# A tower of nine layers: combined projection weights, tile widths in the embedding and the dense experts, order of the gate products

## Chip, cores and metric

One core of one Trainium2 chip. The metric is the device time of one execution in microseconds. Three runs of the kernel before gave 907.95, 909.51 and 910.41; their median is 909.51.

## What is computed

A tower on T = 16 x 36 = 576 tokens of width 256: patch embedding, then four blocks of a sequence mixer and a feed-forward part, all fp32. What the change touches:

```python
# embedding
h = patches @ W.T + b                       # 768 -> 256
# second mixer, a selective state-space layer; x_in is the normed h
x, z = split(x_in @ W_in)                   # W_in 256 x 512
delta_raw, B, C = split(x @ W_x)            # W_x 256 x (256 + 16 + 16)
delta = softplus(delta_raw @ W_dt + b_dt)
h_n = scan(exp(delta * A_n), delta * x * B_n)   # n = 0..15
y = ((sum_n C_n h_n + x * D_param) * silu(z)) @ W_out
# its feed-forward part: 4 experts, all computed for all tokens
n1 = relu(layernorm(x @ W1[e] + b1[e]));  out_e = layernorm(n1 @ W2[e] + b2[e])
# third mixer
act = silu(conv(x_up));  f, i, hidden = grouped 4x4 products of act
# h = scan of functions of f, i, hidden;  out = ((h[-1] + skip * act) * silu(z)) @ w_down
```

## The kernel before

Each engine has its own hand-written program; semaphores join them. Tokens lie in NT = 5 tiles: four of 128 and the last of LAST = 64 (`TILE_N`). PS is PSUM with 8 banks; an fp32 product shows as two instructions in the trace. All products go through `mm` (line 428). `keep_warm(turns, root)` issues 4 idle products of zeros per turn and then waits for the VectorE step of a norm numbered `root`, and issues 5 more. `transpose_x` turns the normed tiles XH into XT (256 x 576, padded to 640 with zeros), which ScalarE's `xt_copy` takes out of PSUM (line 911 or 916) after the norm's square roots (line 901).

Embedding: `products_by_block` (lines 595 to 613) waits for block k of patches and weights and multiplies all five tiles. VectorE waits for the constants (`ld_const`, as do ScalarE at line 997 and GpSimd), adds the bias (1473) and takes statistics (1297).

State-space stage. TensorE (674 to 713): x and z from W_in, B and C from x, delta_raw from x, delta from its copy `dr`, then D_param * x, then the sums over C_n h_n as GpSimd (1229) delivers them. ScalarE (1030 to 1066): copies of x, SiLU of z, copies of B and C (1038), of delta_raw (1042), absolute value (1047), exponential (1050), logarithm (1052), exponential of A_log (1054), then the decays (1064), which it writes to PSUM. VectorE (1581 to 1628) makes softplus from them as max(v,0) + log(1 + exp(-|v|)) with a correction, dx = delta * x, then per state the input (1608) and two scans (1616). SyncE (392 to 406) stores B and C in DRAM when `bc_rows` is 2 and broadcasts them to all partitions, row by row.

Dense experts: per expert, `first_products` (bias of all pairs of tiles, then the tiles from XT), `second_products` of the expert before, `n1_transposes`. VectorE takes statistics (1652), ScalarE normalises (1081, 1092, 1104), GpSimd scales (1237), VectorE adds (1642). The last tile uses 64 columns of the array.

Third mixer: eight projections `up(m)` in two pairs of banks each (x for m < 4, z above), then per m `hidden(m)` and `gates_fi(m)`. HP(m) shares banks with the gates, so `hidden_read` and `gates_read` (VectorE, 1710 and 1715) hold TensorE back, and ScalarE's absolute values (1145), exponential (1147) and logarithm (1149) follow each pair of gates. Then `az_ready` products (840), idle products, `h2_ready` products (845), norm.

Between the embedding and the state-space stage lie a recurrent mixer, a norm (lines 1524 to 1532, TensorE's idle products at line 650) and routed experts. After the third mixer come routed experts, an LRU mixer and routed experts.

## Time and profile before

| | before |
|---|---|
| median of 3 runs | 909.51 us |
| profiled execution | 910.45 us |
| its span, first to last instruction | 908.6 us |
| mean granted TensorE clock | 0.92 of 2.4 GHz |
| TensorE, VectorE, ScalarE, GpSimd busy | 86, 38, 28, 15% of the span |
| embedding | 3.96 to 20.46 |
| first projection to first scan of the state-space stage | 246.15 to 281.13 |
| 16 states of the scan | 281.13 to 338.7 |
| dense experts, first bias to last statistics | 369.54 to 438.3 |
| gates of the third mixer to its output products | 471.57 to 492.94 |

Busy shares are averages over stages with different limits. In the time line, a row gives start and duration in us from the span's start, and in brackets how long the engine had been idle and what released it; PEld are TensorE's weight loads, which run ahead of its products. Rows of equal operations are merged, with their count.

### The profile page before, as it was taken

How to read it: one execution, taken by the hardware profiler on the slowest of the kernel's cores; microseconds unless marked ns; L12 is line 12 of the kernel's file. 1: busy time of each engine (PE TensorE's matmuls, PEld its weight loads, DVE VectorE, ACT ScalarE, POOL GpSimd, SP SyncE). 2: the span in 40 equal slices, each digit the busy share in tenths (PEclk: the TensorE clock that was granted, in tenths of full speed). 3: DMA queues.
4: the chain of work that ended last, by engine and by line, in shares of the span. 5: the costliest groups of instructions: out<-in, count | busy, mean ns of one | idle time of the engine just before them, and what ended most of it. 6: DMA issues, size and time to landing. Idle time of an engine off the chain costs nothing.

```text
span 908.6 us, 13681 instructions
## 1 busy us (share of the span) xinstructions
PE 785.4 (86%) x4875; PEld 599.0 (66%) x4954; DVE 349.3 (38%) x1002; ACT 250.1 (28%) x583; POOL 133.2 (15%) x100
## 2 busy tenths in 40 slices
PE   8878779999972668897896989999998988999997
PEld 5466439988541334564574558999984555999995
DVE  1434650000319996545765742111114551111113
ACT  1222114433243340436166122212220021122221
POOL 1000020000204991012204030000004012000004
PEclk9855889999995999799997979999999979999998
DMA  9500056995132532000000044999954024799972
GB/s 338 219 3 2 1 223 223 323 306 196 32 107 61 152 99 105 1 0 1 0 1 0 1 161 151 321 319 321 323 208 156 0 71 191 231 327 320 320 235 84
DMA packets 39590, 139.27 MB, mean 153 GB/s; under 512 B 5744, under 2 KB 20288, under 8 KB 27904
## 3 DMA queue, kind: packets, MB, share of 16 engines
q1 hardware_dynamic: 37312, 132.88, 43.4%
q0 software_dynamic: 2240, 5.90, 1.9%
q8 instruction: 22, 0.36, 0.2%
q14 instruction: 16, 0.13, 0.0%
HBM read 127.40 MB, written 11.35 MB: 153 GB/s over the span
## 4 chain that ended last, share of the span: by engine, by line
PE 66%; DVE 14%; DMA 5%; issue 5%; ACT 5%; POOL 3%; DVEq 0%; POOLq 0%; SPq 0%; ACTq 0%
PE PS L428 63%; DVE arena L1616 4%; POOL arena L1216 2%; DMA arena<-x_slots 1%; DVE stats L1297 1%; PE PS L485 1%; PE PS L451 1%; POOL arena L1229 1%; DMA arena<-y_slots,posu 1%; DMA arena<-w_moe 1%; ACT arena L1012 1%; DMA x_slots<-XH,posu 1%; ACT XT L911 1%; DMA y_slots<-arena 1%; DMA arena<-bc_scratch 0%
## 5 line engine op out<-in xcount | busy, mean ns | idle before, releaser
L428 PE MATMUL PS<-arena 128*128 128x128 f32 (+4 forms) x3348 | 421.6, 280 | 28.1 <-ACT arena L1012 9.8
L428 PEld LDWEIGHTS PS<-arena 128*128 128x128 f32 (+2 forms) x3348 | 368.7, 172 | 69.5 <-issue 18.3
L428 PE MATMUL PS<-warm 128*128 128x512 bf16 (+1 forms) x397 | 106.4, 379 | 14.8 <-DVE rs L1281 9.0
L1441 DVE TENSOR_TENSOR arena<-arena,PS 128x384 f32<-128x384 f32 (+1 forms) x62 | 30.3, 488 | 199.2 <-ACT arena L949 199.2
L428 PEld LDWEIGHTS PS<-warm 128*128 128x128 bf16 x476 | 46.4, 100 | 66.9 <-DVE rs L1281 12.9
L1216 POOL DMA_INDIRECT arena<-y_slots,posu x25 | 23.9, 954 | 384.6 <-DMA y_slots<-arena 377.9
L949 ACT ACTIVATE arena<-PS 128x384 f32<-128x384 f32 x62 | 30.4, 490 | 162.2 <-PE PS L428 162.2
L428 PE MATMUL PS<-arena,ident 128*128 128x512 f32 (+1 forms) x128 | 39.6, 456 | 38.1 <-POOL arena L1229 38.1
L1229 POOL TENSOR_TENSOR arena<-arena 128x1152 f32<-128x1152 f32 x16 | 56.1, 3509 | 48.8 <-DVE arena L1616 48.4
L1453 DVE SCALAR_TENSOR_TENSOR H<-arena,wgt,H 128x256 f32<-128x256 f32 (+1 forms) x25 | 11.9, 477 | 124.8 <-DMA arena<-y_slots,posu 124.4
L428 PEld LDWEIGHTS PS<-arena,ident 128*128 128x128 f32 x128 | 21.2, 196 | 56.6 <-POOL arena L1229 40.1
L1205 POOL DMA_INDIRECT x_slots<-XH,posu x25 | 24.1, 962 | 194.3 <-DVE posu L1401 187.6
L428 PE MATMUL PS<-XT,wsh 128*128 128x384 f32 (+1 forms) x144 | 43.0, 450 | 0.5 <-ACT arena L962 0.5
L901 ACT ACTIVATE dev<-rs 128x5 f32<-128x5 f32 x19 | 4.1, 216 | 140.5 <-DVE rs L1281 140.5
L1616 DVE TENSOR_TENSOR_SCAN arena<-PS,arena 128x576 f32<-128x576 f32 x32 | 41.6, 1341 | 0.0
L954 ACT ACTIVATE arena<-PS,arena 128x128 f32<-128x128 f32 x96 | 27.4, 368 | 45.5 <-PE PS L428 45.5
L428 PEld LDWEIGHTS PS<-XT,wsh 128*128 128x128 f32 x144 | 28.1, 209 | 13.1 <-issue 4.8
L1064 ACT ACTIVATE PS<-arena 128x560 f32<-128x560 f32 x32 | 23.3, 731 | 41.6 <-DVE arena L1616 37.3
L962 ACT ACTIVATE arena<-PS 128x256 f32<-128x256 f32 x43 | 16.5, 383 | 38.5 <-PE PS L428 38.5
L1237 POOL TENSOR_TENSOR arena<-arena,rowv 128x512 f32<-128x512 f32 (+1 forms) x12 | 13.6, 1158 | 87.5 <-ACT arena L1104 87.5
L428 PE MATMUL PS<-arena,wsh 128*128 128x384 f32 (+1 forms) x72 | 21.6, 426 | 2.9 <-DVE arena L1429 2.9
L485 PE MATMUL PS<-ident,arena 128*128 128x128 f32 x86 | 16.7, 276 | 7.9 <-DMA arena<-x_slots 5.7
(253 smaller groups left out, 756.1 us busy)
## 6 DMA issues: line engine op xcount, KB each, us to landing
arena<-w_moe SPq DMA_DIRECT2D x31, 1152.0 KB, 5.7
arena<-w_moe SPq DMA_DIRECT2D x31, 1024.0 KB, 5.2
arena<-w_moe SPq DMA_DIRECT2D x24, 1026.0 KB, 6.6
...
```

Source lines behind the costliest of these rows:

```text
L428: return nc.tensor.matmul(out_, l, r, start=start, stop=stop, skip_group_check=True)
L485: last = nc.tensor.transpose(PS[:, 6 + p, SB * d:SB * (d + 1)], xslot[p][:, 128 * d:128 * (d + 1)], ident[:, :])
L949: nc.scalar.activation(sg_s[x][:, 0:3 * SB], PS[:, 2 * x, 0:3 * SB], ACT.Silu)\
L954: last = nc.scalar.activation(hid_b[x][:, SB * c:SB * (c + 1)], PS[:, 2 * x, SB * c:SB * (c + 1)], ACT.Silu, bias=wbuf[p][:, o_ + c:o_ + c ...
L962: nc.scalar.activation(y_s[p], PS[:, 4 + p, 0:D], ACT.Copy).then_inc(sem("y_sb"), 1)
L1064: nc.scalar.activation(inner(dA[d]), inner(dl[:, d, :]), ACT.Exp, scale=A_s[:, d, bass.ds(n, 1)])\
L1205: pool.indirect_dma_start(x_slots, bass.IndirectOffsetOnAxis(ap=posu[0:TILE_N[j], k, j:j + 1], axis=0), tile(XH, j), None).then_inc(sem("s ...
L1216: pool.indirect_dma_start(Yg[0:TILE_N[j], k, j * D:(j + 1) * D], None, y_slots[0:SB * NBLK[name], :], bass.IndirectOffsetOnAxis(ap=posu[0: ...
L1229: nc.gpsimd.tensor_tensor(hC[:, n % 2, :, :], hs_[:, n % 2, :, :], bcC[:, n:n + 1, :].to_broadcast([128, KD, T]), ALU.mult)\
L1237: nc.gpsimd.tensor_tensor(u, u, row("g2", D, e)[0:TILE_N[j], None, :].to_broadcast([TILE_N[j], n, D]), ALU.mult)\
L1441: ins = v.tensor_tensor(hid_b[x][:, 0:full], sg_s[x][:, 0:full], PS[:, 2 * x + 1, 0:full], ALU.mult)
L1616: v.tensor_tensor_scan(hs_[:, n % 2, d], dA[d], dBx[:, n % 2, d], 0.0, ALU.mult, ALU.add)\
```

## The change

- Embedding: six idle products first; tiles 0 to 3 by block, the 64-token tile for all blocks at the end.
- State-space stage: TensorE forms W_x' = W_in[:, :256] W_x and W_dt' = W_x'[:, :256] W_dt on the chip, behind the first mixer's output products, in place of 8 of 11 turns of idle products; ScalarE copies them over wx_s and wdt_s. delta, then B and C, then x, then z come from XT. The step-size arithmetic runs in halves of 576 columns; z's copies come behind the first decays, its SiLU behind the loop.
- Dense experts: the last tile and its bias use all 128 columns; n1T is padded with zeros by VectorE.
- Third mixer: HP(m) has banks 2m, 2m+1; ScalarE copies hidden 0 and 1, VectorE 2 and 3; hidden 2 and 3 come before gates 1 to 3.

```diff
@@ -229,6 +229,11 @@
+        winT = YT[:, :, 0:D]
+        def XZ_PS(m):
+            return (PS[:, 0:2] if m else PS[:, 2:4])[:, :, 0:TH]
@@ -243,8 +248,8 @@
-        n1T = part(NT * D, KD, T)
-        eu = part(NT * D + KD * T, 2, NT, D)
+        n1T = part(NT * D, KD, NT * TT)
+        eu = part(NT * D + KD * NT * TT, 2, NT, D)
@@ -261,7 +266,7 @@
-            return PS[:, (0, 4)[m % 2]:(0, 4)[m % 2] + 2, 0:TH]
+            return PS[:, 2 * m:2 * m + 2, 0:TH]
@@ -609,12 +614,20 @@
-            products_by_block(PATCH_K, lambda k: pe.wait_ge(sem(f"ld_patch{k}"), 32),
-                              lambda k, j: patch_s[:, k, tsl(j)], lambda k: wtok_s[:, k, :])
+            pe.wait_ge(sem("warm_ready"), 1)
+            idle_products(6)
+            for k in range(PATCH_K):
+                pe.wait_ge(sem(f"ld_patch{k}"), 32)
+                for j in range(NT - 1):
+                    last = mm(TM(j), patch_s[:, k, tsl(j)], wtok_s[:, k, :], k == 0 and j % 2 == 0, k == PATCH_K - 1)
+                    if k == PATCH_K - 1:
+                        last.then_inc(sem("tm_ready"), 1)
+            for k in range(PATCH_K):
+                last = mm(TM(NT - 1), patch_s[:, k, tsl(NT - 1)], wtok_s[:, k, :], k == 0, k == PATCH_K - 1)
+            last.then_inc(sem("tm_ready"), 1)
...
-            pe.wait_ge(sem("warm_ready"), 1)
@@ -647,7 +660,33 @@
-            keep_warm(11, root=4)
+            def combined_weights():
+                pe.wait_ge(sem("ld_l1a"), 64)
+                for m in range(KD):
+                    for k in range(KD):
+                        last = nc.tensor.transpose(PS[:, 0, D * m + 128 * k:D * m + 128 * (k + 1)],
+                                                   win_s[:, k, 128 * m:128 * (m + 1)], ident[:, :])
+                last.then_inc(sem("wc_psum"), 1)
+                pe.wait_ge(sem("wc_copied"), 1)
+                for q in range(KD):
+                    for m in range(KD):
+                        last = mm(PS[:, 1, D * q:D * (q + 1)], wx_s[:, m, 128 * q:128 * (q + 1)], winT[:, m, :], m == 0, m == KD - 1)
+                last.then_inc(sem("wc_psum"), 1)
+                for k in range(KD):
+                    for m in range(KD):
+                        last = mm(PS[:, 2, 2 * NS * k:2 * NS * (k + 1)], winT[:, m, 128 * k:128 * (k + 1)],
+                                  wx_s[:, m, D:D + 2 * NS], m == 0, m == KD - 1)
+                last.then_inc(sem("wc_psum"), 1)
+                pe.wait_ge(sem("wc_copied"), 2)
+                for k in range(KD):
+                    for q in range(KD):
+                        last = mm(PS[:, 3, D * k:D * (k + 1)], wx_s[:, q, 128 * k:128 * (k + 1)], wdt_s[:, q, :], q == 0, q == KD - 1)
+                last.then_inc(sem("wc_psum"), 1)
+            combined_weights()
+            keep_warm(3, root=4)
+            pe.wait_ge(sem("wc_copied"), 4)
@@ -669,36 +708,26 @@
-            pe.wait_ge(sem("ld_l1a"), 64)
...
-            for m in range(2 * KD):
+            def from_xt(outs, w_of, done):
...
-                        last = mm(PS[:, 4 + 2 * (m % 2) + h, 0:TH], win_s[:, k, 128 * m:128 * (m + 1)], XT[:, k, hsl(h)],
-                                  k == 0, k == KD - 1)
-                last.then_inc(sem("xz_psum"), 1)
+                        last = mm(outs[h], w_of(k), XT[:, k, hsl(h)], k == 0, k == KD - 1)
+                last.then_inc(sem(done), 1)
+            for m in range(KD):
+                from_xt([PS[:, 4 + 2 * m + h, 0:TH] for h in range(2)], lambda k: wdt_s[:, k, 128 * m:128 * (m + 1)], "dt_psum")
+            from_xt([PS[0:2 * NS, h, 0:TH] for h in range(2)], lambda k: wx_s[:, k, D:D + 2 * NS], "bc_psum")
+            for m in range(2 * KD):
...
-                    pe.wait_ge(sem("xz_read"), 2)
...
-            last.then_inc(sem("bc_psum"), 1)
+                    pe.wait_ge(sem("bc_rows"), 2)
+                if m >= 2:
+                    pe.wait_ge(sem("xz_read"), m)
+                from_xt([XZ_PS(m)[:, h, :] for h in range(2)], lambda k: win_s[:, k, 128 * m:128 * (m + 1)], "xz_psum")
...
-            for m in range(KD):
...
-            pe.wait_ge(sem("bc_rows"), 2)
@@ -722,7 +751,7 @@
-                mm(PS[0:TILE_N[j], bank, 0:n * D].rearrange("p (j d) -> p j d", d=D), ones_b[:, 0:TILE_N[j]], b_, True, False)
+                mm(PS[:, bank, 0:n * D].rearrange("p (j d) -> p j d", d=D), ones_b[:, :], b_, True, False)
@@ -731,9 +760,9 @@
-                        z = PS[0:TILE_N[j], q, (j % 2) * D:(j % 2 + 1) * D]
+                        z = PS[:, q, (j % 2) * D:(j % 2 + 1) * D]
...
-                            last = mm(z, XT[:, k, tsl(j)], wl1_s[:, 0, e, k, :], False, k == KD - 1)
+                            last = mm(z, XT[:, k, TT * j:TT * (j + 1)], wl1_s[:, 0, e, k, :], False, k == KD - 1)
@@ -758,9 +787,9 @@
-                        z = PS[0:TILE_N[j], 4 + q, (j % 2) * D:(j % 2 + 1) * D]
+                        z = PS[:, 4 + q, (j % 2) * D:(j % 2 + 1) * D]
...
-                            last = mm(z, n1T[:, k, tsl(j)], wl1_s[:, 1, e, k, :], False, k == KD - 1)
+                            last = mm(z, n1T[:, k, TT * j:TT * (j + 1)], wl1_s[:, 1, e, k, :], False, k == KD - 1)
@@ -776,6 +805,7 @@
+            pe.wait_ge(sem("n1_pad"), 1)
@@ -807,31 +837,29 @@
-                if m < 2:
-                    pe.wait_ge(sem("z_read"), 2 * m + 1)
-                else:
-                    pe.wait_ge(sem("gates_read"), m - 1)
+                pe.wait_ge(sem("z_read"), m + 1)
...
-                pe.wait_ge(sem("hidden_read"), m + 1)
-                if m < 2:
-                    pe.wait_ge(sem("z_read"), 2 * m + 2)
+                pe.wait_ge(sem(("hidden_act", "hidden_dve", "gates_read", "gates_read")[m]), (2, 2, 1, 2)[m])
...
-            for m in range(2 * KI - 1):
+            for m in range(KI + 2):
...
-            up(2 * KI - 1)
+            up(KI + 2)
+            hidden(1)
+            up(KI + 3)
...
+            hidden(2)
+            hidden(3)
...
-                hidden(m)
@@ -1018,7 +1046,19 @@
-            xt_copy("ffn0", "rms_w", norms=3)
+            act.wait_ge(sem("wc_psum"), 1)
+            nc.scalar.activation(winT, PS[:, 0, :].rearrange("p (m i) -> p m i", m=KD), ACT.Copy).then_inc(sem("wc_copied"), 1)
+            square_root()
+            act.wait_ge(sem("wc_psum"), 3)
+            nc.scalar.activation(wx_s[:, :, 0:D], PS[:, 1, :].rearrange("p (q i) -> p q i", q=KD), ACT.Copy)\
+                .then_inc(sem("wc_copied"), 1)
+            nc.scalar.activation(wx_s[:, :, D:D + 2 * NS], PS[:, 2, 0:KD * 2 * NS].rearrange("p (k c) -> p k c", k=KD), ACT.Copy)\
+                .then_inc(sem("wc_copied"), 1)
+            act.wait_ge(sem("wc_psum"), 4)
+            nc.scalar.activation(wdt_s[:, :, :], PS[:, 3, :].rearrange("p (k f) -> p k f", k=KD), ACT.Copy)\
+                .then_inc(sem("wc_copied"), 1)
+            xt_copy("ffn0", "rms_w", norms=2)
@@ -1027,42 +1067,46 @@
-            for m in range(4):
...
-                                     ACT.Copy if m < 2 else ACT.Silu).then_inc(sem("xz_read"), 1)
+            nc.scalar.activation(A_s[:, :, :], colv[:, COL["A_log"]:COL["A_log"] + KD * NS]
+                                 .rearrange("p (k n) -> p k n", k=KD), ACT.Exp).then_inc(sem("A_exp"), 1)
+            for m in range(KD):
+                act.wait_ge(sem("dt_psum"), m + 1)
+                nc.scalar.activation(hs_[:, 1, m].rearrange("p (h t) -> p h t", h=2), PS[:, 4 + 2 * m:6 + 2 * m, 0:TH], ACT.Abs,
+                                     bias=col("b_dt", m)).then_inc(sem("dt_abs"), 1)
+                act.wait_ge(sem("dt_abs"), m + 1)
+                nc.scalar.activation(hs_[:, 0, m], hs_[:, 1, m], ACT.Exp, scale=-1.0).then_inc(sem("dt_e"), 1)
...
-            act.wait_ge(sem("dr_psum"), 1)
...
-            act.wait_ge(sem("dt_psum"), 1)
+            def xz_copy(m):
+                act.wait_ge(sem("xz_psum"), m + 1)
+                dst = xs[:, m, :] if m < 2 else zs[:, m - 2, :]
+                nc.scalar.activation(dst.rearrange("p (h t) -> p h t", h=2), XZ_PS(m), ACT.Copy).then_inc(sem("xz_read"), 1)
...
-                nc.scalar.activation(hs_[:, 1, m].rearrange("p (h t) -> p h t", h=2), PS[:, 4 + m:8:2, 0:TH], ACT.Abs,
...
-                                 .rearrange("p (k n) -> p k n", k=KD), ACT.Exp).then_inc(sem("A_exp"), 1)
+                act.wait_ge(sem("dt_u"), m + 1)
+                nc.scalar.activation(dBx[:, 1, m], dBx[:, 0, m], ACT.Ln).then_inc(sem("dt_ln"), 1)
+                xz_copy(m)
...
-            act.wait_ge(sem("delta_ready"), 1)
...
-            with act.Fori(0, NS) as n:
+            def decays(n):
...
-                    act.wait_ge(sem("delta_ready"), 1)
+                    act.wait_ge(sem("delta_ready"), d + 1)
...
+            decays(0)
+            for m in range(KD, 2 * KD):
+                xz_copy(m)
+            with act.Fori(1, NS) as n:
+                decays(n)
+            nc.scalar.activation(zs[:, :, :], zs[:, :, :], ACT.Silu).then_inc(sem("z_silu"), 1)
@@ -1126,15 +1170,23 @@
-            for m in range(KI):
-                x_copy(m)
+            def hidden_copy(m):
+                act.wait_ge(sem("h_psum"), m + 1)
+                nc.scalar.activation(two(df[:, m, :]), HP(m), ACT.Copy).then_inc(sem("hidden_act"), 1)
...
+            x_copy(0)
+            x_copy(1)
+            x_copy(2)
...
+            x_copy(3)
...
+            z_silu(1)
+            hidden_copy(0)
...
-            z_silu(1)
...
+            hidden_copy(1)
@@ -1150,7 +1202,7 @@
-                act.wait_ge(sem("hidden_read"), m + 1)
+                act.wait_ge(sem("hidden_act" if m < 2 else "hidden_dve"), m % 2 + 1)
@@ -1578,27 +1630,33 @@
-            dve.wait_ge(sem("dt_abs"), KD)
+            ee, u, ln_u = hs_[:, 0], dBx[:, 0], dBx[:, 1]
...
-                mark(v.tensor_scalar(dr[:, m, :].rearrange("p (h t) -> p h t", h=2), PS[:, 4 + m:8:2, 0:TH],
-                                     col("b_dt", m), None, ALU.add))
-            join()
+                dve.wait_ge(sem("dt_abs"), m + 1)
+                v.tensor_scalar(dr[:, m, :].rearrange("p (h t) -> p h t", h=2), PS[:, 4 + 2 * m:6 + 2 * m, 0:TH],
+                                col("b_dt", m), 0.0, ALU.add, ALU.max).then_inc(sem("dt_relu"), 1)
+                dve.wait_ge(sem("dt_e"), m + 1)
+                v.tensor_scalar(u[:, m], ee[:, m], 1.0, None, ALU.add).then_inc(sem("dt_u"), 1)
+                dve.wait_ge(sem("dt_u"), m + 1)
+                link(v.scalar_tensor_tensor(ee[:, m], u[:, m], 1.0, ee[:, m], ALU.subtract, ALU.subtract))
+                dve.wait_ge(sem("dt_relu"), m + 1)
+                mark(v.tensor_tensor(dl[:, m], dr[:, m], ee[:, m], ALU.subtract))
+            dve.wait_ge(sem("A_exp"), 1)
+            v.tensor_scalar(A_s[:, :, :], A_s[:, :, :], -1.0, None, ALU.mult).then_inc(sem("A_ready"), 1)
+            dve.wait_ge(sem("xz_read"), 1)
...
-            ee, u, ln_u = hs_[:, 0], dBx[:, 0], dBx[:, 1]
...
-            dve.sem_inc(sem("scan_half"), 2)
+            for m in range(KD):
+                dve.wait_ge(sem("dt_ln"), m + 1)
+                link(v.scalar_tensor_tensor(ln_u[:, m], u[:, m], 1.0, ln_u[:, m], ALU.is_gt, ALU.mult))
+                v.tensor_tensor(dl[:, m], dl[:, m], ln_u[:, m], ALU.add).then_inc(sem("delta_ready"), 1)
+                if m == 0:
+                    dve.sem_inc(sem("scan_half"), 2)
+            for m in range(KD):
+                dve.wait_ge(sem("delta_ready"), m + 1)
+                dve.wait_ge(sem("xz_read"), m + 1)
+                mark(v.tensor_tensor(dx[:, m], dl[:, m], xs[:, m], ALU.mult))
+            join()
@@ -1626,6 +1684,7 @@
+            dve.wait_ge(sem("z_silu"), 1)
@@ -1634,6 +1693,7 @@
+            v.memset(n1T[:, :, T:NT * TT], 0.0).then_inc(sem("n1_pad"), 1)
@@ -1707,7 +1767,7 @@
-                v.tensor_copy(two(df[:, m, :]), HP(m)).then_inc(sem("hidden_read"), 1)
+                v.tensor_copy(two(df[:, m, :]), HP(m)).then_inc(sem("hidden_dve"), 1)
@@ -1720,13 +1780,10 @@
-            hidden_copy(0)
+            hidden_copy(2)
+            hidden_copy(3)
...
-                if m + 1 < KI and m == 0:
-                    hidden_copy(1)
...
-                if 1 <= m and m + 1 < KI:
-                    hidden_copy(m + 1)
```

## Rows read from the trace of the kernel before

**Rows 1.** The page: clocks granted in 40 slices; shares of the last chain

```profile
PEclk9855889999995999799997979999999979999998
...
PE 66%; DVE 14%; DMA 5%; issue 5%; ACT 5%; POOL 3%; DVEq 0%; POOLq 0%; SPq 0%; ACTq 0%
```

**Rows 2.** Time line, embedding: start us, us, engine, line, operation, tiles, count, [idle<-releaser]

```profile
3.96 3.06 PEld L428 LDWEIGHTS PS<-arena 128*128 128x128 f32 x8 [3.96 <-DMA arena<-w_tok]
...
12.87 0.19 PEld L428 LDWEIGHTS PS<-arena 128*64 128x64 f32 x2 [0.33 <-issue]
...
15.37 0.19 PEld L428 LDWEIGHTS PS<-arena 128*64 128x64 f32 x2 [0.33 <-issue]
...
16.47 0.20 ACT L997 ACTIVATE lru_c<-colv 128x1 f32<-128x1 f32 x1 [14.47 <-DMA gatew<-gate_w]
```

**Rows 3.** Chain in order of time, after the embedding: start us, us, what

```profile
20.48 1.09 DVE H L1473 x3
21.59 1.74 DVE stats L1297 x5
```

**Rows 4.** Time line, TensorE's weight loads in the third block's projections

```profile
452.72 13.39 PEld L428 LDWEIGHTS PS<-XT,arena 128*128 128x128 f32 x56 [0.52 <-issue]
...
466.17 0.92 PEld L428 LDWEIGHTS PS<-arena 128*128 128x128 f32 x4
```

**Rows 5.** Time line, TensorE's idle products before the second norm

```profile
89.95 9.44 PE L428 MATMUL PS<-warm 128*128 128x512 bf16 x33 [0.16 <-issue]
...
102.13 1.25 PE L428 MATMUL PS<-warm 128*128 128x512 bf16 x5 [2.74 <-DVE rs L1281]
```

**Rows 6.** Time line, setup of the state-space stage

```profile
246.15 4.12 PE L428 MATMUL PS<-XT,win_s 128*128 128x288 f32 x16 [0.36 <-ACT XT L911]
...
248.37 0.65 ACT L1034 ACTIVATE arena<-PS 128x576 f32<-128x576 f32 x1 [2.36 <-PE PS L428]
...
255.09 1.59 PEld L428 LDWEIGHTS PS<-arena,wx_s 128*32 128x32 f32 x8 [0.39 <-issue]
...
257.25 0.69 ACT L1038 ACTIVATE arena<-PS 32x288 f32<-32x288 f32 x2 [1.41 <-PE PS L428]
...
281.13 2.60 DVE L1616 TENSOR_TENSOR_SCAN arena<-PS,arena 128x576 f32<-128x576 f32 x2
```

**Rows 7.** Groups by line and shape, 246 to 281.2: busy us, mean ns | idle before

```profile
L1592 DVE SCALAR_TENSOR_TENSOR arena<-arena 128x1152 f32<-128x1152 f32 x1 | 1.4, 1359 | 0.0
...
L1050 ACT ACT_TABLE_LOAD x1 | 1.3, 1283 | 0.0
...
L1050 ACT ACTIVATE arena<-arena 128x1152 f32<-128x1152 f32 x1 | 1.2, 1162 | 0.0
```

**Rows 8.** The four broadcasts of B (line 396): issue to landing

```profile
DMA to landing us min/median/max: 3.2/5.6/6.5
```

**Rows 9.** Time line, one pass of the dense experts

```profile
405.67 0.11 PEld L428 LDWEIGHTS PS<-bias_p,ones_b 128*128 128x128 bf16 x2 [0.39 <-issue]
...
411.09 0.85 PEld L749 LDWEIGHTS PS<-ident,arena 128*128 128x128 f32 x8 [0.38 <-ACT arena L1081]
```

**Rows 10.** Chain in order of time, two steps of the dense experts

```profile
400.31 10.85 PE PS L428 x46
...
413.26 10.85 PE PS L428 x46
```

**Rows 11.** Time line, gate products of the third block and what follows

```profile
471.57 1.19 ACT L1145 ACTIVATE arena<-PS 128x576 f32<-128x576 f32 x2
...
472.79 1.16 ACT L1147 ACTIVATE arena<-arena 128x1152 f32<-128x1152 f32 x1
...
490.11 1.19 ACT L1145 ACTIVATE arena<-PS 128x576 f32<-128x576 f32 x2 [3.62 <-PE PS L428]
...
492.94 11.67 PE L428 MATMUL PS<-arena 128*128 128x256 f32 x40 [2.87 <-DVE arena L1715]
...
508.01 9.97 PE L428 MATMUL PS<-arena 128*128 128x256 f32 x40
```

40 lines of the change are left out of this document (removed).

## Prediction

> **What bounds the kernel now.** I read the page first: its chain of work that ended last is two thirds TensorE, the rest VectorE, DMA and ScalarE, and its row of granted clocks shows stretches of half speed [rows 1]. The shares are averages over nine stages, so the stages that the change touches were read one by one: the time line, to see on which engine each gap ends, then the chain in order of time. They give four different limits. The embedding is TensorE alone: one row of it runs from 3.96 without a gap [rows 2], and VectorE's last three additions and the statistics follow [rows 3]. The setup of the state-space stage is a relay: from the first projection at 246.15 to the first scan at 281.13 pass 34.98 us, in which TensorE, ScalarE and VectorE wait for one another [rows 6]. The dense experts are TensorE for 10.85 of every 12.95 us [rows 10]. The gate products of the third block are a ring of three engines, four turns from 471.57 to the next stage at 492.94 [rows 11]. What these stages lose or gain reaches the end in full: each hands its result to a layer norm on which all later work waits, and the later stages are unchanged.
>
> **Embedding.** Five tiles of tokens, the last of 64, are multiplied block by block. An fp32 product is two instructions, so a block is 10. One block runs from 12.87 to 15.37, 2.50 us [rows 2]. In a row of products of one width 56 instructions of 288 columns take 466.17 - 452.72 = 13.45, 0.240 each [rows 4]; by columns that is 0.2135 for 256, and 2.13 for ten. A block with the narrow tile in it so pays 0.37 for turning to 64 columns and back. The change does the narrow tile for all blocks at the end. In front come six idle products of 512 columns, between the zeroing of their operand (about 1.3 us) and the arrival of the first block at 3.96; the first eight weight loads took 3.06, so nearly twice the later pace, and I take 2.1 for them with the engine already busy (bounds: eight at 0.2135, 1.7; and 3.5). Sum: 3.96 + 2.1 + 5 x 1.71 + 12 x 0.2135 + 0.2 for one turn = 17.4. The constants land at 16.47 [rows 2]; the additions of tiles 0 to 3 run from there at 0.36 each [rows 3] and the last ends at 18.4, where statistics started at 21.59. **Gain 3.1**, between 1.5 (cold start, blocks arriving late; then it is DMA that is next) and 3.2 (the constants bound it).
>
> **Combined weights.** W_in's first half times W_x, and that times W_dt, are now formed on the chip: 4 transposes, 4 products of 256 columns, 4 of 32, 4 of 256, and four copies on ScalarE, in place of 32 of the 44 idle products behind the first mixer. VectorE works alone there until 102.13, where TensorE's idle products came to an end at 99.4 and it sat idle for 2.74 [rows 5]. At the upper clock: transposes to 91.2, copy to 91.9, 16 instructions to 94.9, copy to 95.6, 8 to 97.4, copy to 98.0, twelve idle ones to 100.0: cover 2.1 us. ScalarE has nothing else there but a root of 0.2. I book **0**; the bounds are a gain of 1.5, if a shorter idle time leaves the transposes at 103.9 at the upper clock, and a loss of 4.1, if all of it runs at the lower one (rival 3). The wait for the four weight loads moves here from 246; they were issued by 12.5, and this is at 90.
>
> **State-space setup.** Before: x, then B and C, then the low projection, a copy, the step-size projection, six serial steps over 1152 columns. After: the step size comes straight from XT, so TensorE starts with it. Times in the frame of before, from 246.15:
> - TensorE: the two halves of dt are 16 instructions of 288 columns, 3.84; the first half is on ScalarE at 248.37, as x was [rows 6]. B and C follow; their copies lay 257.25 - 255.09 = 2.16 behind the load [rows 6], now 250.1 + 2.2 = 252.4, and are done at 253.1. x, first half, 8 instructions behind them, arrives at 254.5.
> - ScalarE: absolute value and exponential of each half, 0.65 to 0.75 each, end at 249.8 and 251.7; B and C copies 253.1; a table load of 1.28, whose follower starts with no idle time [rows 7]; logarithm and x copy of half 0 to 255.75; of half 1 to 257.1; load, first decays 258.4 to 259.9.
> - VectorE: dt's bias, u, e - u and their difference, per half at most 0.77 + 3 x 0.68 (half of 1.36, [rows 7]), run from 249.1 to 254.6, in the shadow. It then waits for the x copy at 255.75 (the zeros of the decays share its bank), then six steps of 0.7 to 260.1 and two inputs of 1.36: first scan at 263.0.
> - SyncE: B and C leave for the scratch at 253.2; the broadcasts start 1.7 later and land 3.2 to 6.5 after issue [rows 8]: B0 by 258, B1 by 260 to 262.3, against a need at 261.7. Late next after VectorE, by at most 0.6.
>
> 281.13 - 263.0 = **18.1**, bounds 14 and 18.5. z's two halves are copied behind the first decays; TensorE has them at 262.5, ScalarE is free at 263.2, and the second decays are wanted at 264.3: 1.1 of cover. z's SiLU moves behind the loop, where ScalarE idles. The 16 turns of the loop are VectorE's, unchanged.
>
> The Trainium skill (ScalarE: Activation LUTs, What ACT_TABLE_LOAD costs) gives each switch a drain of 1.38 behind the 1.28. By it the two switches in the new relay would cost 2.8 more on ScalarE. The rows show no such idle time, so the trace decides.
>
> **Dense experts.** The last tile is computed 128 wide, on zeros. From a bias load to the transposes behind the products lie 411.09 - 405.67 = 5.42 us [rows 9], for 1280 bias columns (0.53) and 20 instructions of 256 (4.27): 4.80 without turns. So 0.6 is lost in each pass. There are 8; the first is partly at the lower clock (0.5), and in the last the biases are paced by ScalarE (0.35). The step of 12.95 becomes 10.85 - 1.2 + 2.1 [rows 10], as VectorE's and ScalarE's part starts 0.6 earlier too; the added zeroing of 128 columns is over before the logits. Sum 0.5 + 6 x 0.6 + 0.35 = **4.4**, bounds 1.8 (only 0.1 for each narrow product and for each bias) and 4.8.
>
> Against it the Trainium skill (TensorE: Matmul & The Clock Gate, LDWEIGHTS) lets a weight load cost its columns over 1.2 GHz. Doubling the narrow ones adds an estimated 0.053 us to each of 32, 1.7 in all, if they lay open. In a row of one width they don't: 0.240 is the columns' own time [rows 4].
>
> **Gate products.** Before, a copy, the gates' absolute values and two VectorE steps stood between one turn and the next. After, all four hidden products have banks of their own. TensorE: eight projections, hidden 0 and 1, gates 0 are 80 instructions, over at 472.3 as before; hidden 2 and 3 to 474.3, VectorE's copy to 475.1, gates 1 to 477.2. ScalarE, 1.19 + 1.16 + 1.16 a turn [rows 11]: absolute values at 472.4, 477.2, 480.8, 484.4. Then 1.19 and two VectorE steps of 0.77: the next stage at 487.15 instead of 492.94, **5.8** earlier. What follows is TensorE's and moves with it; its start at the lower clock (40 instructions in 11.67 against 9.97 later, [rows 11]) stays. ScalarE's hidden copies fit between waits. Bounds 3 (a SiLU or copy in the new order late by one projection, and the clock down longer) and 6.5.
>
> **Sum.** 3.1 + 0 + 18.1 + 4.4 + 5.8 = 31.4. The profiled execution took 910.45, with a span of 908.6; that makes 879.05 and 877.2. It lies 0.94 above the median of the runs; on the median I forecast **878.1**.
>
> **Rivals.**
> 1. The turns are cheap (the row shows only 0.1 where a full pair of loads follows) and the first block stays cold: 1.5 + 18.1 + 1.8 + 5.8 = 27.2, so 882.3. Against it: the two rates of rows 2 and 4.
> 2. The new relay is slower than drawn: ScalarE holds nine steps in one order, and one that is late moves all. With the x copies behind both logarithms' waits, broadcasts at 6.5, and z on the second decays, it gives 14: 882.2.
> 3. The combined weights end up on the path: all at 1.2 GHz, TensorE reaches the transposes at 107.9 instead of 103.86: 4.1 back, 882.2. For it: half a microsecond's gaps for each copy; against it: 16 products in a row, and 2.1 of cover.
> 4. Slower than before: the shift sets TensorE's idle gaps otherwise, and the long routed stages, which are bound by it, run at 1.2 GHz where they had 2.4. A microsecond there costs half of one, so it decides from 63 us more of it. The mean of 0.92 means some 145 us below now. At 80 us more: 909.5 - 31.4 + 40 = 918. Against it: those stages have 9s in the row of clocks [rows 1], and nothing in them is changed.
> 5. It doesn't do what it says: the next late thing takes the whole gain of one part, as when the first scan waits for something unseen. Half of 31.4: 894.
>
> **Chances.** Forecast 0.62 (875 to 881), rival 1 0.13, 2 0.10, 3 0.06, 5 0.07, 4 0.02. Between the bounds of all parts the gain is 1.5 - 4.1 + 14 + 1.8 + 3 = 16 and 3.2 + 1.5 + 18.5 + 4.8 + 6.5 = 34.5; not all ends meet, so the range is 874 to 887, which leaves out 4, 5 and some of what combines. 0.3% is 2.7 us, about what measuring this kernel can tell from no change: faster 0.97, same 0.01, slower 0.02.
>
> **What would show it.** Statistics at 18.4; no 128*64 loads in the experts and a step of 11.7; idle products over before the root at about 99; 17 us from first projection to first scan; absolute values of the gates 3.6 apart. It is wrong if the first scan comes later than 20 us after the projections, if TensorE is the releaser of the first transposes of the second norm, or if the steps of the experts stay above 12.5.

## The result and the profile after

The changed kernel takes 878.67 us (median of 4 runs, 873.46 to 886.24), the kernel before beside it 908.73 (4 runs, 904.72 to 910.41): a ratio of 0.968, 95% interval 0.9637 to 0.9722. In two more series the ratio was 0.9611 (0.9554 to 0.9668) and 0.9659 (0.9629 to 0.9689). The forecast was 878.1, with a range of 874 to 887. So the total was met, by 30.1 us of gain in the medians against 31.4 in the sum. Two of its terms were not met, in opposite directions: the experts gave 7.2 us where 4.4 were booked, the gates 3.5 where 5.8 were. Most of what follows is about them.

The profiled execution after took 880.7, with a span of 878.9. The clocks granted in 40 slices, and the shares of the last chain, against [rows 1]:

```profile
PEclk9855889999999999899989899999999888999998
...
PE 60%; DVE 13%; DMA 11%; issue 5%; ACT 5%; POOL 3%; SPq 1%; DVEq 0%; POOLq 0%; ACTq 0%
```

TensorE's share of the chain fell from 66% to 60%, DMA's rose from 5% to 11%. Behind the first six slices the row before had a 5 (273 to 295 us: end of the setup, first scans) and four 7s, among them one in the experts (363 to 386 us); after, nothing there is below 8.

**Embedding** (against rows 2 and 3). TensorE's weight loads (start us, us, engine, line, operation, count, idle before), and then the chain:

```profile
3.88 2.46 PEld L433 LDWEIGHTS PS<-arena 128*128 128x128 f32 x8 [0.74 <-DMA arena<-w_tok]
6.61 8.50 PEld L433 LDWEIGHTS PS<-arena 128*128 128x128 f32 x40 [0.28 <-DMA arena<-w_tok]
15.45 2.35 PEld L433 LDWEIGHTS PS<-arena 128*64 128x64 f32 x12 [0.33 <-issue]
```

```profile
9.19 7.88 DMA gatew<-gate_w
...
17.10 1.75 DVE H L1525 x5
...
18.87 1.73 DVE stats L1349 x5
```

The narrow tile's twelve instructions stand in one row. TensorE is past them at 18.2 (17.4 in the sum), and the statistics start at 18.87 in place of 21.59: 2.7 earlier. As the bound said, the constants are now next late; they arrived at 17.10.

**Second norm** (against rows 5). TensorE's idle products:

```profile
94.01 2.54 PE L433 MATMUL PS<-warm 128*128 128x512 bf16 x9
99.54 1.25 PE L433 MATMUL PS<-warm 128*128 128x512 bf16 x5 [2.99 <-DVE rs L1333]
```

The combined weights are over before 94.01, the norm is still released by VectorE's root (`DVE rs`), and TensorE waits 2.99 where it waited 2.74. They cost nothing.

**State-space setup** (against rows 6). TensorE's first two groups, VectorE's last steps:

```profile
240.57 4.15 PE L433 MATMUL PS<-XT,wdt_s 128*128 128x288 f32 x16 [0.27 <-ACT XT L939]
244.65 2.13 PE L433 MATMUL PS<-XT,wx_s 128*32 128x288 f32 x8
```

```profile
250.12 0.74 DVE L1651 SCALAR_TENSOR_TENSOR arena<-arena 128x576 f32<-128x576 f32 x1
...
254.49 2.63 DVE L1666 TENSOR_TENSOR arena<-arena 128x1152 f32<-128x1152 f32 x2
257.03 2.60 DVE L1674 TENSOR_TENSOR_SCAN arena<-PS,arena 128x576 f32<-128x576 f32 x2
```

From first projection to first scan: 257.03 - 240.57 = 16.46 us, where it was 34.98. VectorE waited 0.98 for ScalarE's copy of x and is busy without a gap from 250.12 on: it bounds the start of the scans, as drawn. (The chain names a broadcast there, landing at 256.95, so 0.08 us ahead of the scan. VectorE had no idle time, so it was not late, but a faster VectorE would gain no more than these 0.08.)

**Dense experts** (against rows 10), two steps of the chain:

```profile
371.30 9.82 PE PS L433 x46
...
383.06 9.83 PE PS L433 x46
```

The step is 11.76 (11.75 in the sum), where it was 12.95.

**Gates** (against rows 11). ScalarE's absolute values, and what follows on TensorE:

```profile
439.93 1.19 ACT L1197 ACTIVATE arena<-PS 128x576 f32<-128x576 f32 x2
...
444.82 1.19 ACT L1197 ACTIVATE arena<-PS 128x576 f32<-128x576 f32 x2 [1.30 <-PE PS L433]
...
448.31 1.17 ACT L1197 ACTIVATE arena<-PS 128x576 f32<-128x576 f32 x2
...
451.77 1.17 ACT L1197 ACTIVATE arena<-PS 128x576 f32<-128x576 f32 x2
```

```profile
454.58 12.46 PE L433 MATMUL PS<-arena 128*128 128x256 f32 x40 [4.73 <-DVE arena L1775]
```

Four turns are 4.9, 3.5, 3.5 and 2.8 apart (4.8, 3.6, 3.6, 2.7 in the sum). The next stage begins 34.44 us behind the first projection, where it was 40.22: 5.8 less.

By these landmarks the two profiled executions differ so, 29.7 us in all: 2.7 in the embedding, 0.2 lost at the second norm, 3.0 in the first routed stage, 18.5 in the setup, 0.6 at the fourth norm, 8.0 in the experts, 5.0 from there to the norm of the next routed stage, 0.7 lost up to the seventh norm, and 7.2 lost from the last norm to the end. The experts gave more than booked, and the end, in which nothing was changed, lost.

### The profile page after: what moved, and what is told of

It is laid out like the page before. It is cut to its first block, busy times and chain, and to the rows that moved or that the text cites. A ratio compares the mean times of both kernels' runs of the same rounds, so it can differ in the third digit from the quotient of the medians.

```text
span 878.9 us, 13652 instructions
## 1 busy us (share of the span) xinstructions
PE 771.4 (88%) x4869; PEld 598.1 (68%) x4940; DVE 348.2 (40%) x1007; ACT 253.7 (29%) x590; POOL 132.8 (15%) x100
## 4 chain that ended last, share of the span: by engine, by line
PE 60%; DVE 13%; DMA 11%; issue 5%; ACT 5%; POOL 3%; SPq 1%; DVEq 0%; POOLq 0%; ACTq 0%
PE PS L433 57%; DVE arena L1674 4%; DMA arena<-w_moe 3%; DMA arena<-x_slots 3%; POOL arena L1268 2%; DVE stats L1349 1%; PE PS L490 1%; DMA arena<-bc_scratch 1%; PE PS L456 1%; POOL arena L1281 1%; DMA arena<-y_slots,posu 1%; DMA gatew<-gate_w 1%; SPq L319 1%; ACT arena L1040 1%; DMA x_slots<-XH,posu 1%
## 5 line engine op out<-in xcount | busy, mean ns | idle before, releaser
L433 PE MATMUL PS<-warm 128*128 128x512 bf16 (+1 forms) x379 | 102.7, 384 | 15.9 <-DVE rs L1333 9.4
L433 PEld LDWEIGHTS PS<-warm 128*128 128x128 bf16 x450 | 44.2, 101 | 65.5 <-DVE rs L1333 13.2
L977 ACT ACTIVATE arena<-PS 128x384 f32<-128x384 f32 x62 | 30.4, 490 | 169.1 <-PE PS L433 169.1
L990 ACT ACTIVATE arena<-PS 128x256 f32<-128x256 f32 x43 | 16.5, 383 | 38.5 <-PE PS L433 38.5
L490 PE MATMUL PS<-ident,arena 128*128 128x128 f32 x86 | 17.4, 286 | 7.7 <-DMA arena<-x_slots 5.5
L433 PE MATMUL PS<-arena,wsh 128*128 128x384 f32 (+1 forms) x72 | 21.6, 426 | 2.9 <-DVE arena L1481 2.9
```

What stands on the lines that cost most here:

```text
L433: return nc.tensor.matmul(out_, l, r, start=start, stop=stop, skip_group_check=True)
L490: last = nc.tensor.transpose(PS[:, 6 + p, SB * d:SB * (d + 1)], xslot[p][:, 128 * d:128 * (d + 1)], ident[:, :])
L977: nc.scalar.activation(sg_s[x][:, 0:3 * SB], PS[:, 2 * x, 0:3 * SB], ACT.Silu)\
L990: nc.scalar.activation(y_s[p], PS[:, 4 + p, 0:D], ACT.Copy).then_inc(sem("y_sb"), 1)
```

## The experiments

Twelve more runs were made, two of them of the changed kernel again. For each, one execution was profiled; its stretches are set side by side here (us). All limits are instructions that every kernel has: "setup" runs from the third norm's first copy into XT (ScalarE) to the first scan, "experts" from the first product (or its weight load) with the experts' weights to the next norm's copy into XT, "gates" from the first projection of the third block to the table load behind the gates, "behind" from there to the next norm's copy, "end" from the last norm's copy to the end.

| kernel | first XT | second to third XT | setup | experts | gates | behind | end |
|---|---|---|---|---|---|---|---|
| before | 26.38 | 139.36 | 36.54 | 80.48 | 40.99 | 29.6 | 176.4 |
| after | 23.66 | 136.40 | 17.93 | 72.53 | 35.24 | 30.4 | 183.6 |
| r1 after again | 24.02 | 135.20 | 17.93 | 75.23 | 35.24 | 30.6 | 178.0 |
| r2 embedding alone | 23.62 | 135.74 | 36.55 | 80.51 | 38.73 | 29.6 | 176.8 |
| r3 combined alone | 26.96 | 135.32 | 17.97 | 80.45 | 38.73 | 29.6 | 179.0 |
| r4 experts alone | 27.07 | 138.05 | 36.55 | 73.13 | 39.42 | 29.6 | 178.9 |
| r5 gates alone | 26.06 | 136.48 | 36.55 | 80.52 | 35.24 | 29.6 | 178.4 |
| r6 all but experts | 24.32 | 133.94 | 17.93 | 80.87 | 35.25 | 29.6 | 180.5 |
| r7 no warm start | 25.47 | 133.23 | 17.93 | 73.14 | 35.25 | 30.5 | 181.0 |
| r8 longer warm | 23.85 | 132.91 | 17.93 | 73.22 | 35.25 | 30.5 | 179.4 |
| r9 after, third | 24.05 | 135.94 | 17.93 | 73.39 | 35.25 | 30.5 | 178.3 |
| r10 ranks' gaps filled | 23.51 | 132.70 | 17.93 | 72.77 | 35.24 | 30.5 | 182.7 |
| r11 two gaps filled | 23.83 | 133.42 | 17.93 | 71.78 | 35.24 | 28.0 | 178.2 |
| r12 all filled | 23.62 | 133.09 | 17.93 | 71.63 | 35.24 | 28.0 | 183.0 |

**1. The same kernel again.** No edit.

> The changed kernel itself, so that the parts are weighed beside it on one chip. Its gain came out at 30 us instead of 31.4, and two stages don't match the sum: the stage of the dense experts was 4 us better than worked out, and the last routed feed-forward (739.76 to 852.74) lost 7 us to waits for the weight transfers. Theory 1, the loss varies from execution to execution: the time lies at 875 to 886, and the last routed feed-forward of this trace lasts anything between 106 and 114 us. Theory 2, the loss belongs to the change (the weights are fetched at another phase): the stretch lasts 112 to 114 us again, with waits of 7 us or more for w_moe.

Measured: 877.8 us (874.84 to 882.02) against 910.35. The end took 178.0 us, where the same kernel had taken 183.6. Leaving out experiments 10 and 12, which put idle products into this stretch, all profiles have the same code there, and it took 176.4 to 183.6. The stretch in whole, of the profiled execution after, of this one, and of the kernel before (us; busy time and instructions of TensorE, its weight loads, VectorE, ScalarE, GpSimd; the mean granted clock, DMA share, GB/s):

```profile
695.29:878.87 183.58, 168.24 (x1060) 145.37 (x1058) 38.73 (x123) 35.28 (x80) 18.98 (x20) 0.94 0.65 220
```

```profile
702.22:880.18 177.96, 163.51 (x1060) 142.75 (x1058) 38.72 (x123) 35.12 (x80) 18.99 (x20) 0.96 0.68 227
```

```profile
732.18:908.59 176.41, 164.15 (x1060) 143.13 (x1058) 38.74 (x123) 35.07 (x80) 18.97 (x20) 0.95 0.67 229
```

Theory 1 holds for most of it: the stretch varies from execution to execution. But the waits for weights, to which the expectation lays the loss, are not what differs. Of the 5.6 us between the two executions of the changed kernel, 4.7 are TensorE busy for longer with the same 1060 instructions (168.24 against 163.51), at a mean granted clock of 0.94 against 0.96; the time in which it is not busy differs by 0.9, and its waits for `w_moe` are 1.8 and 1.6. The GB/s are the same bytes over the two lengths, and explain nothing. Against the kernel before, of the 7.2 us 4.1 are busy time and 3.1 are not. How much of those 7.2 is the change stays open: the four kernels without the combined weights took 176.4 to 178.9 at the end (before, 2, 4, 5), the eight with them, 10 and 12 again left out, 178.0 to 183.6. The means are 2.1 us apart.

**2. The embedding alone.**

```
-            products_by_block(PATCH_K, lambda k: ..., lambda k, j: patch_s[:, k, tsl(j)], lambda k: wtok_s[:, k, :])
+            pe.wait_ge(sem("warm_ready"), 1)
+            idle_products(6)
+            ... blocks over tiles 0 to 3, then all blocks of tile 4
```

> The kernel before with the embedding part alone (twelve narrow loads, warm-up first, products in the new order). My sum: first statistics 2.7 to 3.1 us earlier, the rest unchanged, so 2.7 to 3.1 us faster than the kernel before. Rival: a gain ahead of the routed stages is swallowed by the wait for the expert weights, which are fetched at their own time: then the time is within 1 us of the kernel before although the first statistics come 2.7 us earlier.

Measured: 907.28 against 910.35, ratio 0.9976 (0.9943 to 1.0009), and the first XT at 23.62. Over all profiles the first XT comes at 26.06 to 27.07 without this part and at 23.51 to 24.32 with it and the warm start. In the means (26.6 and 23.8) that is a gain of 2.8. The time agrees (3.1), but its interval holds zero as well, so the time alone decides nothing between the sum and the rival. The stretches speak against the rival: the next two are no longer than in other kernels.

**3. The combined weights and the setup alone.**

```
+            combined_weights()
+            keep_warm(3, root=4)
...
-                last.then_inc(sem("dr_psum"), 1)
+                from_xt([...], lambda k: wdt_s[:, k, 128 * m:128 * (m + 1)], "dt_psum")
```

> The kernel before with the combined weights and the short state-space setup alone. My sum: first scan about 18.5 us after the first projection's start is saved, transposes of the second normalisation unmoved, 17.5 to 19 us faster. Rival, what is saved there is partly given back in the second routed feed-forward by waits for w_moe: 11 to 14 us faster, with the loss in the last 150 us of the trace.

Measured: 894.82 against 910.35, 15.5 us, ratio 0.9818 (0.9763 to 0.9872; that is 11.7 to 21.6 us). The setup is 17.97 in place of 36.54, to 0.04 us the same in every kernel that has this part, and the time from the first XT to the second is 79.15. Without this part it was 78.85, 79.06, 79.06 and 80.51 (before, 2, 4, 5), with it 78.8 to 80.1 in the other profiles: a cost of making the weights can't be told from this scatter. The setup's 18.6 is in the interval of the time; the rival, part of it given back at the end, isn't excluded, since the lower end of the interval is 11.7 and this kernel's end took 179.0 against 176.4.

**4. The full-width experts alone.**

```
-                mm(PS[0:TILE_N[j], bank, 0:n * D].rearrange("p (j d) -> p j d", d=D), ones_b[:, 0:TILE_N[j]], b_, True, False)
+                mm(PS[:, bank, 0:n * D].rearrange("p (j d) -> p j d", d=D), ones_b[:, :], b_, True, False)
... and the products' operands likewise 128 tokens wide
```

> The kernel before with the full-width dense experts alone (128 columns of every product, also in the last tile). My sum from the column counts: 4.4 us. The trace of the changed kernel showed 8.6 in this stage. If the full width itself brings more than I worked out (the switches of the tile's width cost more than I took), the gain is 7 to 9 us with the granted clock of the stage as in the kernel before. If 4 of the 8.6 came from the granted clock falling for a shorter time, at another phase of the kernel, this kernel shows the old dips and gains 4 to 5 us.

Measured: 904.72 against 910.35, ratio 0.9921 (0.9894 to 0.9948), so 4.7 to 9.6 us; the stage 73.13 in place of 80.48. It reaches the experts when the kernel before does (369.7 against 370.7 us) and still gains 7.35.

**5. The gates alone.**

```
-            gates_fi(0)
-            hidden(2)
...
+            hidden(1)
+            up(KI + 3)
+            gates_fi(0)
+            hidden(2)
+            hidden(3)
+            for m in range(1, KI):
+                gates_fi(m)
```

> The kernel before with the gate part alone (the gate products of the third block in one run with their functions' tables loaded less often). My sum said 5.8 us, and the traces of before and after differ by 5.75 from the first gate product to the table load behind the gates (40.99 us before, 35.24 after). But the kernels that left the gates alone took 38.73, 38.73 and 39.42 us there, with shorter stretches at the lower clock than the profiled run of before. Theory 1, the part is worth what I summed, 5 to 6 us. Theory 2, 2.3 us of it was the lower clock in the profiled run of before, from whose rows I worked: this kernel shows 35.2 us in that stretch and is 3 to 4 us faster than the kernel before in the mean of many runs.

Measured: 906.6 against 909.99, 3.4 us, ratio 0.9953 (0.9924 to 0.9981). That is 1.7 to 6.9 us and holds both theories; the stretches decide between them. (The tables are not loaded less often, as the expectation says: both orders have three loads there.) The stretch is 35.24, as in every kernel with this part. What it replaces took 38.73 twice, 39.42 and, in the profile that I had, 40.99. Two rows of ScalarE's absolute values in run 2, the third and the fourth turn:

```profile
475.67 1.19 ACT L1153 ACTIVATE arena<-PS 128x576 f32<-128x576 f32 x2 [3.05 <-PE PS L428]
...
481.40 1.19 ACT L1153 ACTIVATE arena<-PS 128x576 f32<-128x576 f32 x2 [2.15 <-PE PS L428]
```

In the profile before, the fourth waited 3.62 [rows 11], and the third 3.84. Theory 2: from the first turn to the fourth pass 16.27 here and 18.54 there, and the 2.3 between them are these two waits of ScalarE for TensorE. Over the whole stretch TensorE had 7.7 us at 1.2 GHz there and 4.5 here.

**6. All but the experts.** The changed kernel with the hunk of experiment 4 taken back.

> The changed kernel with the dense experts' tiles left at 64 columns in the last block. It reaches the experts at the phase of the changed kernel. If the narrow tile itself makes the lower clock last longer, the stretch from the first product of the expert stage to the next normalisation takes 79 to 81 us with 17 us or more of it at the lower clock, as in the three kernels that had narrow tiles, against 72.5 to 75.2 us with 10.2 to 13.7 in the three that had full ones; the whole is then 6 to 8 us slower than the changed kernel. If the phase decides, the stretch takes 76 to 78 us with 10 to 14 us at the lower clock, and the whole is 4 to 5 us slower.

Measured: 884.85 against 909.99 (ratio 0.9721, 0.9651 to 0.9792), a gain of 25.1 where the changed kernel gained 30.1 to 32.5. The stage is 80.87. Its first 20 us and then the rest, beside run 4 (columns as above; the clock is the third from the end):

```profile
344.38:364.38 20.00, 17.85 (x65) 12.24 (x64) 9.98 (x45) 7.19 (x16) 0.00 (x0) 0.74 0.00 1
364.38:394.38 30.00, 28.47 (x131) 19.19 (x130) 18.49 (x84) 15.51 (x38) 6.33 (x6) 1.00 0.00 1
394.38:425.25 30.87, 24.37 (x101) 13.64 (x100) 19.06 (x62) 10.03 (x24) 7.24 (x6) 0.89 0.00 1
```

```profile
369.76:389.76 20.00, 17.85 (x78) 13.38 (x77) 11.82 (x57) 7.27 (x17) 0.00 (x0) 0.83 0.00 1
389.76:419.76 30.00, 26.79 (x139) 22.14 (x137) 20.11 (x88) 20.01 (x49) 6.35 (x6) 1.00 0.00 1
419.76:442.79 23.03, 18.13 (x79) 10.17 (x80) 15.29 (x48) 5.40 (x15) 7.23 (x6) 0.93 0.00 0
```

This settles width against phase, the time at which the kernel reaches the stage. Five kernels with the narrow tile took 80.45 to 80.87, though they came to the stage at anything between 344 and 371 us; seven with full tiles took 72.5 to 75.2, 73.3 in the mean (and two with a gap filled, below, 71.6 and 71.8). The width is worth 7.2. From the clocks of the rows, 2 x ((1 - 0.74) x 20 + (1 - 0.89) x 30.87) = 17.2 us of run 6's stage were at 1.2 GHz, and 2 x ((1 - 0.83) x 20 + (1 - 0.93) x 23.03) = 10.0 of run 4's. By the same working the other narrow ones had 17 us, and the kernel before 20; the full ones 10, and run 1 14. The full width shortens the time at the lower clock by 7 us as a rule, at either phase. Why the clock is granted otherwise, the rows don't tell: the loads and products are as many, only wider.

**7. Without the idle products at the start.**

```
             pe.wait_ge(sem("warm_ready"), 1)
-            idle_products(6)
```

> The changed kernel without the six idle products at the start. If the embedding's products pay for a cold start, they end later than the constants arrive (17.1 us) and the first copy into XT comes 0.5 to 1.5 us later than 23.7. If the start is bound by the loads, as the chain says, the first copy into XT comes within 0.3 us of 23.7 and the time is that of the changed kernel.

Measured: 882.37 (ratio 0.9689, 0.9622 to 0.9757), first XT at 25.47, 1.6 later than in the mean of the kernels with them. The chain of this kernel shows TensorE where the constants were:

```profile
4.97 15.23 PE PS L433 x59
...
20.68 1.73 DVE stats L1348 x5
```

By this one profile the idle products are worth more than half of the embedding's gain. In the prediction that was the lower bound of 1.5, "cold start": here it is 26.6 - 25.5 = 1.1, against the mean of the four kernels without this part. The time line shows what they do: without them the weight loads start 0.43 us apart until 9.46 and 0.22 apart from there; in the kernel after, behind idle products from 1.30 on, that half pace ends at 5.71. The profile's granted clock reads 1.00 over both pieces, so this slow start can't be seen in it.

**8. A longer filling behind the combined weights.**

```
-            keep_warm(3, root=4)
+            keep_warm(7, root=4)
```

> The changed kernel with seven turns of idle products behind the combined weights in place of three, so that they end at about 99.5 instead of 96.6 us, when the second normalisation releases the next ones. If the transposes of the second normalisation (0.64 us a pair, at the lower clock in both kernels) pay for that gap, they take about half and the logits come 1 to 2 us earlier than 105.4. If the gap is not what keeps the clock low there, the transposes keep their 0.64 us and nothing moves, or the idle products end after 99.5 and cost up to 0.5 us.

Measured: 873.27 against 909.99, ratio 0.9574 (0.951 to 0.9639). TensorE ahead of the second norm's transposes, and the first of them:

```profile
94.32 7.29 PE L433 MATMUL PS<-warm 128*128 128x512 bf16 x33
101.89 0.41 PE L456 MATMUL PS<-ident,XH 128*128 128x128 f32 x2 [0.28 <-DVE XH L1359]
```

A pair of transposes takes 0.38 to 0.41 where it took 0.64 in both kernels. (In run 7, with the same gap of 2.99 unfilled, only the first pair took 0.63, the others 0.38 to 0.39: what the gap costs differs from one execution to the next.) The logits come only 0.6 earlier (104.78 against 105.37, though this execution was 0.2 later at the first XT), since the copies into XT set the pace then. The gain on the kernel before is 36.7 us, where the changed kernel had 30.1 to 32.5 in its three series. The second to third XT is 132.91, against 135.2 to 136.4 in the three profiles of the changed kernel. I had not expected that, and can't put it down to this edit alone, since runs 6 and 7 show 133.9 and 133.2 without it; but all four kernels with this filling lie at 132.7 to 133.4.

**9. The changed kernel beside its versions.** No edit.

> The changed kernel once more, beside three versions of it. 875 to 880 us. By the traces so far its stages repeat to 0.3 us (17.93 us from the second normalisation's XT to the first scan, 67.2 to 67.4 us behind the gates), and the two parts that don't are the stretches in which routed blocks wait for weights (177 to 184 us at the end) and the expert stage (72.5 to 75.2 us, by one more stretch of 3.4 us at the lower clock).

Measured: 881.47 (879.1 to 883.18) against 913.75. The stages repeated as said.

**10. The gaps ahead of the ranks filled,** and the filling of experiment 8.

```
+                idle_products(6)
                 pe.wait_ge(sem("masks"), STAGE[name] + 1)
```

> The changed kernel with seven turns of idle products behind the combined weights and six idle products in each of the three gaps between the gate logits and the ranks (2.4 to 2.55 us, ended by the masks of VectorE). In the traces each gap is followed by 7 to 10 us at the lower clock in the shared experts. If TensorE's idleness in the gap brings the clock down, the lower stretches behind 492 and 702 us are gone or halved and each saves 2 to 4 us; the kernel is 3 to 8 us faster than the changed one. If the clock falls there for another reason, the stretches stay as they are and the time is within 2 us of it.

Measured: 876.45, ratio 0.96 (0.9557 to 0.9643), 5.0 less than run 9. In the profiles 3.2 of it lie between the second and third XT (132.70 against 135.94), where both experiment 8's filling and the first of these gaps are; the run can't part them. Of the two lower stretches behind the later gaps one stayed and one went: the first 16 us behind the norm of each, first in this kernel, then in run 9 (columns as above).

```profile
484.45:500.45 16.00, 14.91 (x62) 9.56 (x61) 8.44 (x52) 5.14 (x8) 3.44 (x4) 0.79 0.26 81
694.39:710.39 16.00, 13.66 (x66) 8.68 (x65) 8.50 (x52) 5.14 (x8) 3.89 (x4) 1.00 0.28 97
```

```profile
486.85:502.85 16.00, 13.18 (x56) 9.11 (x55) 8.38 (x52) 5.14 (x8) 3.45 (x4) 0.79 0.25 78
698.91:714.91 16.00, 13.18 (x57) 9.08 (x56) 8.60 (x52) 5.15 (x8) 3.43 (x4) 0.79 0.25 81
```

The expectation of 2 to 4 us for each fell. What TensorE still waited for the masks was 0.83 us where the clock fell and 1.24 where it stayed up, so the length of what is left of the gap doesn't decide it. The end took 182.7 all the same, against 178.3 in run 9: at the higher clock (0.97 against 0.96) TensorE was not busy for 18.1 us of it, against 14.9. The longest of these waits, 4.17 us behind a VectorE product, stands in run 9 as well (4.12); what made the others longer stays open.

**11. Two longer gaps filled,** and the filling of experiment 8.

```
+                if e == E1:
+                    idle_products(15, 0)
...
+            pe.wait_ge(sem("gates_read"), KI - 1)
+            idle_products(14, 0)
+            mm(PS[:, 0, 0:512], warm[:, 0:128], warm[:, 0:512]).then_inc(sem("az_warm"), 1)
             pe.wait_ge(sem("gates_read"), KI)
...
             act.wait_ge(sem("gates_read"), KI)
+            act.wait_ge(sem("az_warm"), 1)
```

> The changed kernel with seven turns behind the combined weights, fifteen idle products in the gap of 4.73 us ahead of the products behind the gates (they follow at the lower clock, 6.8 us long) and fifteen in the gap of 3.50 us ahead of the last expert's second products (3.4 us at the lower clock follow). If the gaps bring the clock down, the expert stage loses its stretch at 53 us (72.5 to 73.2 us becomes 71 to 72) and the one behind the gates goes too; what the latter is worth depends on whether the down products wait for VectorE anyway: 0 to 3 us. In all 1 to 5 us faster than the changed kernel. If the clock falls for another reason, no change within 1 us.

Measured: 875.78 (871.8 to 879.76), ratio 0.9596 (0.9561 to 0.9631), 5.7 less than run 9. TensorE behind the gates in this kernel:

```profile
447.34 3.41 PE L433 MATMUL PS<-warm 128*128 128x512 bf16 x15 [1.26 <-DVE arena L1781]
450.80 10.07 PE L433 MATMUL PS<-arena 128*128 128x256 f32 x40
```

The same 40 products took 12.46 in the changed kernel, behind a gap of 4.73; now 10.07. The whole stretch from the gates to the next norm shrank by 2.5, all of it on the path, and the experts by 1.6 (73.39 to 71.78). For both gaps the first theory holds, in the stretches.

**12. All of it, and the gate weights off the list of constants.**

```
-            load(gatew[:, :, :, :], gate_w, "const")
+            load(gatew[:, :, :, :], gate_w, "gatew")
... and the waits for the constants from 16 * 6 to 16 * 5
```

> The changed kernel with all of these fillings, and with the gate weights off the list of constants for which VectorE waits at the start (17.10 us now; without them the wait ends at the fifth constant, some 0.5 us earlier, and the last embedding product at about 18 us is next late). If the pieces add: 4 to 12 us faster than the changed kernel, so 866 to 875 us, with the first statistics 0 to 0.5 us earlier. If a filled gap only moves the lower stretch to the next place, less than the sum of the two kernels before it.

Measured: 876.36 (870.44 to 878.65), ratio 0.9581 (0.9545 to 0.9617). The first XT came at 23.62, 0.2 to 0.4 earlier than in runs 8 and 9. But run 10 had 23.51 without this edit, so it shows nothing for it. Nothing came on top of run 11: the pieces don't add in the time, though the experts (71.63) and the stretch behind the gates (28.0) keep theirs; the end took 183.0. Against the changed kernel beside them, runs 10 to 12 are 5.0, 5.7 and 5.1 us faster, which the runs don't tell apart from one another. But experiment 8's filling alone had 36.7 us on the kernel before in its series, and these three have 37.3, 38.0 and 37.4 in theirs. So the longer filling behind the combined weights may carry all that the time shows; the 4.1 us of experiment 11 are shown in its stretches, not in the time.

## Why the prediction was right, and where it wasn't

**Embedding, 3.1 booked (its own times, 21.59 - 18.4, give 3.2), 2.7 to 2.8 measured.** Right in kind. The first eight loads took 2.46, where I took 2.1; TensorE is over at 18.2, not 17.4, and the constants arrive at 17.10, not 16.47. The gain stayed inside its bounds of 1.5 and 3.2. The price of a turn, 0.37 a block, is what the sum rests on: with full tiles only, 40 loads took 8.50, 0.2125 each, as worked out from the 0.2135 of a row of one width.

**Combined weights, 0 booked.** Right: no cost stands out of the scatter of 78.8 to 80.5 us between the first two XTs. The cover was drawn as 2.1 and is 2.99: TensorE was past them at 94.0 plus twelve idle products. Rival 3 (all of it at 1.2 GHz) did not come up. The upper bound, transposes at the upper clock, took four more turns of idle products (experiment 8), and was worth 0.6 to the logits, not 1.5.

**Setup, 18.1 booked, 18.5 measured** (18.6 from XT). It lies at the upper bound of 18.5. The relay was drawn step by step, and its times hold within 0.4: B and C copied by 6.96 behind the first projection (6.95 drawn), x's first half by 9.5 (9.6), first scan at 16.46 (16.85). VectorE bounds it, as said, and the broadcasts are the next late thing, as said, by 0.08 us. The drain that the Trainium skill (ScalarE: Activation LUTs, What ACT_TABLE_LOAD costs) gives each switch doesn't show here either: three tables are loaded on this path, and behind each the next operation follows at once, as in these rows of the kernel after:

```profile
240.54 1.28 ACT L1070 ACT_TABLE_LOAD   x1
241.83 0.23 ACT L1070 ACTIVATE arena<-colv 128x32 f32<-128x32 f32 x1
```

**Experts, 4.4 booked, 7.2 measured** (5 profiles against 7), above the upper bound of 4.8. The term for the turns was right: the undisturbed step fell by 1.19, 0.6 for each pass, and the Trainium skill's longer weight loads (TensorE: Matmul & The Clock Gate, LDWEIGHTS) stayed hidden, since 1.19 is what the sum gives without them (1.2). What failed was a step that wasn't there: I priced widths at the clock of the rows and held the clock fixed. It isn't. The full width took 7 us off the time at 1.2 GHz (17 against 10). Half of that is 3.5; with 4.4 it would make 7.9, somewhat above the 7.2. Between the changed kernel's two extremes (72.5 and 75.2) the rows show one more stretch at the lower clock, at the stage's start.

**Gates, 5.8 booked, 3.5 measured against the usual case.** The new ring was drawn rightly, to 0.2 us over four turns (11.84 against 12.0 from first to last). The old one was taken from one execution, in which TensorE was at the lower clock for longer than in the three others profiled since (40.99 against 38.73, 38.73 and 39.42). So 2.3 of the 5.75 that the two profiles differ by are a property of that execution. The failed step is the subtraction: I took the old time from rows with a low clock in them, and the new one at full clock, and did not ask whether the low clock was part of the ring.

**The sum.** 2.8 + 0 + 18.6 + 7.2 + 3.5 = 32.1, against 30.1, 32.5 and 32.3 in the medians of three series. One interplay is seen: with full experts and new gates together the stretch behind the gates is 0.9 longer (30.5, at a mean granted clock of 0.93 in experiment 7, against 29.6 at 0.94 and 0.96 in experiments 4 and 6). That 31.4 was so close was luck: the experts' +2.8 and the gates' -2.3 nearly cancelled; the parts alone were measured at 3.1, 15.5, 5.6 and 3.4, together 27.6, each within a few us.

**Rivals.** 1 (turns are cheap) fell with the step of 11.76. 2 and 3 fell with the setup and the second norm. Of 4, the reverse was seen: the clock did move with the change, but upward. 5 did not come up. The three signs that would have shown it wrong stayed away: the first scan came at 16.5, VectorE released the second norm, the step was under 12.5.

**Left open.** Why the first routed stage takes 132.7 in some kernels and 139.4 in another is not settled. The kernel before had the longest of 14; the four kernels without the combined weights have a mean of 137.4 and the six with them and the short filling 135.0, so some 2.4 us of the total may be in there, with a reason that I haven't found. Nor is it settled whether the 2.1 us by which the same four are shorter at the end is chance. In the total the two would about cancel.
